# First attention of a four-stage transformer kernel: an 80-row head stack without cleared rows, and projections that wait for each group of weights by itself

## The reference

```
x = x + attn_a(layernorm(x))   # 16 heads; 16 content + 64 rotary rows of q and k per head
x = x + ffn(layernorm(x))      # 8 experts, the best 2 of each token
x = x + attn_b(layernorm(x))   # 32 heads, 8 key/value heads
x = x + ffn(layernorm(x))
```

```
c_q = x @ w_dq.T;  c_kv = x @ w_dkv.T                 # 192 and 64 columns
q_c = c_q @ w_uq.T; k_c = c_kv @ w_uk.T; v = c_kv @ w_uv.T   # 16 per head
q_r = c_q @ w_qr.T; k_r = x @ w_kr.T                  # 64 per head, then rotated by position
q = concat(q_c, q_r); k = concat(k_c, k_r)            # 80 per head
out = softmax(q @ k.T / sqrt(80) + causal mask) @ v;  out @ w_out.T
```

## Time and profile before

| | |
|---|---|
| median of 3 runs | 920.73 us (919.67 to 921.72) |
| profiled execution | 918.71 us, span 916.5 us |
| PE busy | 794.6 us (87%) |
| DVE, ACT, POOL busy | 365.2, 290.3, 224.1 us |
| chain that ended last | PE 80%, DVE 8%, DMA 5%, issue 2% |

### The profile page before, as it was taken

One profiled execution on the slowest core, in us unless ns is written; L12 is line 12 of the kernel. 1 busy time (PEld: TensorE's weight loads), 2 busy tenths in 40 slices (PEclk: granted clock), 3 DMA queues, 4 the chain that ended last, 5 costly groups with the idle time before them and its releaser, 6 DMA issues.

```text
span 916.5 us, 14815 instructions
## 1 busy us (share of the span) xinstructions
PE 794.6 (87%) x5020; PEld 604.0 (66%) x5021; DVE 365.2 (40%) x902; ACT 290.3 (32%) x527; POOL 224.1 (24%) x260
## 2 busy tenths in 40 slices
PE   1989799999989999999955389989897999999990
PEld 0767677777767677777744257767664767777760
DVE  8445154543633322222236476676543421221212
ACT  1101203114233343433313214445463234334321
POOL 8351004333131511211223400011302421211212
PEclk9999899999999999999986779999998999999995
DMA  6962913213963216100221631211311111001004
GB/s 185 415 144 83 330 78 86 65 39 94 353 201 90 64 35 232 40 24 33 63 69 41 196 80 34 52 43 41 128 39 57 58 35 34 29 29 34 29 18 143
DMA packets 48123, 88.09 MB, mean 96 GB/s; under 512 B 8913, under 2 KB 37329, under 8 KB 45937
## 3 DMA queue, kind: packets, MB, share of 16 engines
q1 hardware_dynamic: 36743, 54.56, 21.2%
q0 software_dynamic: 7568, 30.97, 9.2%
q10 hardware_dynamic: 3760, 1.87, 0.7%
HBM read 52.04 MB, written 35.03 MB: 95 GB/s over the span
## 4 chain that ended last, share of the span: by engine, by line
PE 80%; DVE 8%; DMA 5%; issue 2%; ACT 2%; POOL 1%; SPq 0%; ACTq 0%; POOLq 0%; DVEq 0%
PE bank L1388 24%; PE bank L1415 13%; PE bank L883 9%; PE bank L462 4%; PE bank L507 4%; PE bank L1401 4%; PE bank L518 2%; PE bank L452 2%; PE bank L536 2%; PE bank L505 2%; PE bank L579 2%; DVE stat L327 2%; DVE XN L599 1%; DMA PTR<-rows_out 1%; PE bank L553 1%
## 5 line engine op out<-in xcount | busy, mean ns | idle before, releaser
L1388 PE MATMUL bank<-wgu,R 128*128 x736 | 225.5, 459 | 0.5 <-ACT R L1423 0.4
L1388 PEld LDWEIGHTS bank<-wgu,R 128*128 128x128 f32 x736 | 137.8, 193 | 65.9 <-issue 3.7
L1415 PE MATMUL bank<-R 112*128 (+1 forms) x552 | 127.0, 379 | 1.2 <-ACT R L1437 1.2
L1415 PEld LDWEIGHTS bank<-R 112*128 112x128 f32 (+1 forms) x552 | 104.4, 190 | 22.3 <-issue 1.7
L1453 DVE TENSOR_TENSOR R<-R,bank 128x344 f32<-128x344 f32 x92 | 47.1, 512 | 180.4 <-PE bank L1388 169.8
L650 ACT ACTIVATE PTR<-bank 128x512 f32<-128x512 f32 x144 | 83.5, 597 | 98.8 <-PE bank L507 83.3
L1364 POOL DMA_INDIRECT rows_out<-R,XN x46 | 45.8, 996 | 169.4 <-ACT R L1445 157.8
L1460 DVE COPY R<-bank 112x512 f32<-112x512 f32 x46 | 31.7, 690 | 103.8 <-PE bank L1401 103.8
L599 DVE TENSOR_REDUCE XN<-bank 128x2 f32<-128x512 f32 x96 | 63.1, 684 | 11.0 <-PE bank L462 11.0
L1431 ACT ACTIVATE R<-bank 128x344 f32<-128x344 f32 x92 | 41.8, 457 | 76.8 <-PE bank L1388 76.6
L1445 ACT ACTIVATE R<-bank 128x256 f32<-128x256 f32 x46 | 17.7, 384 | 146.8 <-PE bank L1415 146.8
(11 more groups left out here) (167 smaller groups left out, 1284.1 us busy)
## 6 DMA issues: line engine op xcount, KB each, us to landing
wgu<-in_wgu SPq DMA_DIRECT2D x10, 1376.0 KB, 11.3
slots_in<-PTR POOLq DMA_DIRECT2D x1, 9088.0 KB, 26.1
row_of_slot<-in_unused POOLq DMA_DIRECT2D x2, 4544.0 KB, 17.8
R<-slots_in SPq DMA_DIRECT2D x46, 128.0 KB, 2.0
wgu<-R SPq DMA_DIRECT2D x32, 128.0 KB, 2.4
R<-R SPq DMA_DIRECT2D x32, 128.0 KB, 2.4
PTR<-rows_out SPq DMA_DIRECT2D x16, 256.0 KB, 3.2
R<-in_wd SPq DMA_DIRECT2D x8, 448.0 KB, 6.0
```

The lines of the kernel that those rows point to most:

```text
L1388: last = nc.tensor.matmul(BK[2 * half + gu][:, 0:IH], xsT[:, p, kk, :], wgu[:, bass.ds(e * (KD * GU) + (kk * GU + gu * I + half * IH), IH) ...
L1415: last = nc.tensor.matmul(down_bank(i)[:, 0:D], hT[0:CH[c], p, c, :], wd[0:CH[c], bass.ds(e * (6 * D) + c * D, D)], start=c == 0, stop=c == 5)
```

## The change

The rotary rows stand at rows 16 to 79 instead of 32 to 95, so a stack has 80 rows (`RA`), and no row needs a zero. The two clearings on POOL go, the count that ACT and POOL wait for goes from 5 to 3, and SP's wait for it goes. The six weights of s_wc are split: `wkr` alone (s_wk), `wuq`, `wuk`, `wuv` (s_wu), `wqr` and `woa` (s_wc), and PE waits for each before the items that use it. The four semaphores of x become two: the first part alone, and parts 1 to 3 together.

```
-RA = 96
+RA = HDA + RD
...
-        s_x = [sem(f"s_x{b}") for b in range(B)]
+        s_x = [sem("s_x0"), sem("s_x123")]
+        s_wk = sem("s_wk")
+        s_wu = sem("s_wu")
...
-                        nc.sync.dma_start(dst[32 + 32 * a:64 + 32 * a, j:HA:4, :],
+                        nc.sync.dma_start(dst[HDA + 32 * a:HDA + 32 + 32 * a, j:HA:4, :],
...
-        INIT = 5
+        INIT = 3
...
-            for dst, src in ((wkr, "wkr"), (wuq, "wuq"), (wuk, "wuk"), (wuv, "wuv"), (wqr, "wqr"), (woa, "woa")):
+            sp.dma_start(wkr, dr["wkr"]).then_inc(s_wk, 16)
+            for dst, src in ((wuq, "wuq"), (wuk, "wuk"), (wuv, "wuv")):
+                sp.dma_start(dst, dr[src]).then_inc(s_wu, 16)
+            for dst, src in ((wqr, "wqr"), (woa, "woa")):
                 sp.dma_start(dst, dr[src]).then_inc(s_wc, 16)
-            sp.wait_ge(s_init, INIT)
...
-            pool.memset(R1[0:32, 0:2 * HA * S], 0.0).then_inc(s_init, 1)
-            pool.memset(room(EVEN, 2 * HA * S)[0:32, :], 0.0).then_inc(s_init, 1)
             pool.wait_ge(s_init, INIT)
-            pool.wait_ge(s_wc, 16 * 6)
+            pool.wait_ge(s_wc, 16 * 2)
...
-            norm_vector(0, lambda b: (s_x[b], 16))
+            norm_vector(0, lambda b: (s_x[0], 16) if b == 0 else (s_x[1], 16 * 3))
...
-            pe.wait_ge(s_wc, 16 * 6)
-            project_a_tensor(0, range(2, ITEMS))
+            pe.wait_ge(s_wk, 16)
+            project_a_tensor(0, range(2, 6))
+            pe.wait_ge(s_wu, 16 * 3)
+            project_a_tensor(0, range(6, 9))
+            pe.wait_ge(s_wc, 16 * 2)
+            project_a_tensor(0, range(9, ITEMS))
```

More of the change, by code:

```diff
@@ L1619, in _ @@
             for t in range(0, NT, 2):
-                sp.dma_start(xres[:, t:t + 2, :], xd[:, t:t + 2, :]).then_inc(s_x[t // 2], 16)
+                sp.dma_start(xres[:, t:t + 2, :], xd[:, t:t + 2, :]).then_inc(s_x[min(t // 2, 1)], 16)
             for dst, src in ((ident[:, :], "ident"), (identb[:, :].bitcast(U16), "identb"), (masks[:, :, :].bitcast(U16), "masks"),
```

## The result

The changed kernel takes 932.35 us (median of 4 runs, 930.52 to 933.45) beside 920.2 us for the kernel before in the same comparison (4 runs, 919.53 to 921.72): a ratio of 1.0154, 95% interval 1.0129 to 1.018. It is 12 us slower; 919.1 us had been predicted. The profiled execution took 930.52 us with a span of 928.6 us, against 918.71 and 916.5 before.

A forecast was written before the change was run, and what follows sets the result against it. PE bounds the kernel, idle at the start while POOL's clearings stall DVE. 10.0 (stalls) - 5.3 (placing held back) - 3.0 (clock) = 1.7, called 1.6, less than 920.73 gives 919.1 us; range 914.0 to 922.6.

The forecast's parts named there:

- The clearings and DVE: At the start, DVE's two L327 stalls behind POOL's clearings go; PE's first matmul comes at 9.3, 10.0 us earlier.
- Merging x's semaphores: At the start, DVE's second group waits for parts 1 to 3; costs PE at most 0.6 us.
- The split weights, 0: At PE's items 2 to 12, separate weight semaphores: nothing counted, since PE's time there is not on the path.
- The bound of 2.1 us: At item 2, the most PE would wait for the weights with one semaphore: 21.3 - 19.2 us.
- SP's placing: SP's 32 issues of sequence 0 run from 29.3 to 59.1, slow until 46.9; PE's first scores start at 62.6.
- 5.3 (placing held back): Before sequence 0's scores, the long transfer slows the placing, taking 5.3 us of the 10.0 gained.
- The bound of 1.84 us: Slowest pace per placing issue under the long transfer: 9 issues at that pace, PE's first scores at 65.1.
- The page on DMA queues: Bears against the long hold of the placing: by its rule the result lies toward the not-held-back rival, 910.7 us.
- The first rival: While POOL's second clearing ran, loads were slowed; without it `woa` and the long transfer come 3.3 us earlier: 916.9, chance 0.22.
- So the price is 7.0 - 0.95 - 3.1 = 3.0 us: Sequence 0's first scores run at 1.2 GHz after PE's new 6.7 us wait, costing 3.0 us.
- 80 rows instead of 96: no matmul or weight load has fewer columns, ... so 0: In the stacks, fewer rows change no matmul columns and no transfer count or size: 0, kept at +-0.4 us.
- The slower rival: At PE's wait before sequence 0's scores, PE resumes at 66.2: 1.1 gained, 3.2 lost to the clock, 922.8, chance 0.15.

The follow-up runs named there:

- the idle-matmul kernel: Changed kernel with 40 unused matmuls on PE before the first scores: seven runs from 914.21 to 919.51 us, four from 930.13 to 932.94.
- the kernel with both transfers late with 80 rows: Changed kernel, 9088 KB transfer issued behind sequence 0's placing, 4544 KB one inside sequence 2: 908.09 us, eight runs 905.5 to 910.2, four 917.1 to 918.4.
- the best schedule with 80 rows: Changed kernel, 9088 KB transfer issued behind sequence 0's placing, 4544 KB one directly behind sequence 1's: 898.46 us, ratio 0.9795 to the kernel before.

## Why the prediction was wrong, step by step

Right, with small errors, and what the rivals came to:

- The clearings and DVE. L327's stalls are gone, and DVE's two-element additions take 0.17 us. PE's first matmul came at 8.90 (predicted 9.3), so the start gained 10.45 us, not 10.0. Merging x's semaphores cost DVE 1.59 us of idle time before 6.68, but `rope`, for which PE waits too, landed only at 8.63, so the merge cost PE 0.3 us at most (0.6 allowed).
- The split weights, 0: shown by undoing it, for this kernel, whose later wait covers it. The bound of 2.1 us was low: undone, PE waited 3.7 us before item 2.
- SP's placing starts at 28.83 (29.3). It was slow until about 48 (46.9), with 11 issues done by then (13), and ended at 61.2 (59.1). PE resumed at 64.7 (62.6) and waited 9.1 us (6.7). The direction and the mechanism are right, and moving the long transfer away shows them. So the term "5.3 (placing held back)" came to 7.8. The pace was too good: the 1.32 us per issue of the nearest row came from 6.6 us of overlap at the end of the long transfer, and the issues further inside took 1.4 to 2.4 us each. The bound of 1.84 us named for this term gave 9 issues and PE at 65.1, nearer to what came.
- The page on DMA queues: the Trainium skill, "DMA: Bandwidth & Descriptors", section Queues, rings and completion order, says that a DMA engine takes turns between its queues packet by packet. Once the two queues share, the trace agrees in its counts (377 to 379). A packet of that page holds several descriptors, and no run shows whether the profile's packet of 9 KB, which the prediction took for it, is the same. The row that spoke against the page, queue 0 alone for 5 us, is also real and comes first. Equal counts still give a queue of 1 KB packets a tenth of the time beside 9 KB packets, so turns and a long hold go together.
- The first rival was wrong. The long transfer did leave 1.9 us earlier, since `woa` landed 8.9 us after its issue instead of 10.7. But in the profiled execution of the changed kernel run again `woa` took 10.8 us, so this differs from execution to execution of one kernel. The loads of 11.5 to 18 us ran at 191 GB/s without the clearing, as they did with it (187):

```profile
11.50:18.00 6.50, 6.50 (x22) 3.80 (x21) 2.00 (x9) 1.07 (x3) 0.00 (x0) 1.00 0.84 191
```

  The Trainium skill, "SBUF — State Buffer", section SBUF: two separate sides, had said that engine and DMA ports can't contend; the two numbers agree with it.

Wrong, and it is 11.4 of the 13.4 us by which the profiled execution (930.52) missed the forecast for it (917.1): the term "So the price is 7.0 - 0.95 - 3.1 = 3.0 us", the clock behind the new wait. It measured 14.4 us (11.6 in the scores and 2.75 in items 11 and 12). With 3.0 in its place the measured rows would have given 918.71 - 2.6 + 3.0, about 919; the other 2 us are the placing. For matmuls over 96 rows the 3.0 was about right: in the changed kernel with 96 rows the wait of 8.03 us cost 2.4.

The reason lies in another line of the same sum, "80 rows instead of 96: no matmul or weight load has fewer columns, ... so 0". Instruction for instruction that is right: at either clock a score matmul takes as long over 80 rows as over 96. The price of 3.0 us was taken from matmuls over 96 rows, and was applied to matmuls over 80. The two terms were worked out apart, the rows as a matter of columns and placing, the wait as one that costs what such a wait cost before, and neither asked whether the part of the change that seemed free had changed the conditions of the other. The experiments show that it is the two together. Rows alone: +0.2%. The rest of the change with its new wait, at 96 rows: +0.2%. Both: +1.5 to +1.7%.

The slower rival named the right place (PE's wait before the scores of sequence 0) and the right kind of cost, with the point from which it decides at 64.3 and PE in fact at 64.68. Its price, 3.0 to 3.4 us, had the same fault, so the range ended at 922.6. (Its sum has a slip: from 29.3 to 48 at 1.84 us ten issues fit, not nine, which gives 922.2 instead of 922.8.) The clock row of the page before stands at 9 in slices 3 and 4 and could not show it; nothing in the trace of before had a low clock over an 80-row matmul. What could have been seen is that no row bounded this price from above for 80 rows: the 12.4 us of scores at half the clock throughout, another 12.4 us, belonged into the range.

What stays open: what in the work decides whether the clock returns (only 80, 88 and 96 rows were tried, only for float32 score matmuls, and in both operands at once), why the clock falls in some executions and not in others behind a wait of 2 to 3 us, why the idle-matmul kernel and the kernel with both transfers late with 80 rows fall into two groups of runs, and why the best schedule with 80 rows doesn't.

## What to carry to other kernels

When a change creates or lengthens a wait of the bounding engine, price the clock by what runs behind the wait, in its changed form, and if the trace has no row for that form, take the whole stretch at half the clock as the upper bound, up to the next work for which a row exists. A gain at the start of a kernel only counts as far as the transfers between it and the next consumer move too: here a long transfer of no urgency, issued at the start, took 8 of 10 us back, and with it and its smaller companion issued later the kernel is 20 us faster than before, with either layout. Narrower operands aren't free just because each instruction takes the same time.

## What the runs showed of the hardware that was not expected

- After a wait of 7 to 9 us, score matmuls in float32 over 80 or 88 rows ran at the 1.2 GHz level for 24 us and more, with PE busy 99% of the time (the low stretch was 57.6 to 95.1 us in the changed kernel). The same matmuls over 96 rows, 16 of them zeros, were back at 2.4 GHz 5.0 us after PE resumed. The clock of the slow kernels came back 3.9 to 6.7 us after PE had gone on to other float32 matmuls over 96 rows (six traces).
- The clock was also seen low as PE resumed after a wait of 2.44 us that followed 8.8 us of dense matmuls, and after one of 2.85 us; after the waits of 1.38 us before the first scores it was up.
- A clearing of 32 x 8192 elements on POOL (6.9 us) held a DVE instruction of 2 elements per partition for 6.5 to 6.7 us; without it, 0.17 us.
- A queue that starts while another queue's long transfer runs got no packet in 30 to 33 us, then as many as the other (377 beside 379 in 10 us). SP's issues rise from 0.6 us to as much as 2.4 us under such a load.
